# V as three one-pass products, graph 0 in another order, and L's first two tiles one behind the other

## What is computed

```python
def hypergraph_conv(x, adj, W, b):
    H = (adj != 0).astype(x.dtype)
    w = adj.reshape(N, -1)[:, :C]                 # the first row of adj
    xw = jnp.einsum('ncd,hd->nch', x, W)
    Dn = jnp.einsum('nce,ne->nc', H, w);  Dn = jnp.where(Dn > 0, 1.0 / Dn, 0.0)
    Be = H.sum(axis=1);                   Be = jnp.where(Be > 0, 1.0 / Be, 0.0)
    m = Be[:, :, None] * jnp.einsum('nce,nch->neh', H, xw)
    return Dn[:, :, None] * jnp.einsum('nce,neh->nch', H, m) + b

h = jax.nn.relu(hypergraph_conv(x, adj, W1, b1))
y = hypergraph_conv(layer_norm(h, gamma, beta), adj, W2, b2) + x
x = _layernorm(x + y)
agg = jnp.einsum('bij,bjf->bif', adj, x) / jnp.maximum(deg, EPS)
x = _layernorm(x + relu(concatenate([x, agg]) @ WL.T))
```

## Time and profile before

| | us |
|---|---|
| median of 3 runs | 1089.8 (1089.41 to 1090.03) |
| the profiled execution | 1090.12 |
| its span | 1088.5 |
| PE busy | 1073.5 (99%) |
| DVE, ACT, POOL busy | 746.4, 372.7, 217.5 |
| granted TensorE clock | 0.999 in the mean (2.4 GHz) |

### The profile page before, as it was taken

The page is one execution under the profiler, slowest core; times in us unless marked ns, Lnnn a source line. Parts: engine busy times, 40 slices in busy tenths (PEclk is TensorE's granted clock), DMA queues, the critical chain, the costliest instruction groups (busy, mean ns, idle before and its releaser), DMA issues.

```text
span 1088.5 us, 18849 instructions
## 1 busy us (share of the span) xinstructions
PE 1073.5 (99%) x6235; PEld 919.3 (84%) x6235; DVE 746.4 (69%) x1972; ACT 372.7 (34%) x811; POOL 217.5 (20%) x276
## 2 busy tenths in 40 slices
PE   7899999999999999999999999999999999999997
PEld 7789698896988969898798978989789896888966
DVE  6875596665965768758687486774867747867326
ACT  5372213622145321453115431154302533026230
POOL 1623004220041202312032120411204120041000
PEclk9999999999999999999999999999999999999999
DMA  8207712076210662125611355115542065300001
GB/s 295 59 1 156 155 42 57 0 154 155 57 40 24 130 157 55 39 54 121 143 48 39 83 126 117 41 39 112 128 87 68 9 142 127 68 11 1 1 1 39
DMA packets 63871, 86.44 MB, mean 79 GB/s; under 512 B 8164, under 2 KB 53864, under 8 KB 63848
## 3 DMA queue, kind: packets, MB, share of 16 engines
q1 hardware_dynamic: 63376, 85.75, 34.4%
q10 hardware_dynamic: 472, 0.40, 0.1%
HBM read 77.73 MB, written 8.39 MB: 79 GB/s over the span
## 4 chain that ended last, share of the span: by engine, by line
PE 91%; DVE 6%; DMA 1%; issue 1%; ACT 0%; SPq 0%; DVEq 0%
PE bank L882 41%; PE bank L993 10%; PE bank L1056 10%; PE bank L975 10%; PE bank L912 8%; PE bank L1023 3%; PE bank L1028 3%; PE bank L1029 3%; PE bank L1001 3%; PE bank L1041 1%; DMA raw<-in_adj_dram 1%; DVE adjT L666 1%; DVE unread L618 1%; DVE HT L671 1%; DVE m_lo L653 1%
## 5 line engine op out<-in xcount | busy, mean ns | idle before, releaser
L882 PE MATMUL bank<-yv,adjT 128*128 128x257 f32 x1024 | 223.3, 379 | 0.0
L882 PEld LDWEIGHTS bank<-yv,adjT 128*128 128x128 f32 x1024 | 193.6, 189 | 31.8 <-issue 3.8
L469 ACT ACTIVATE small<-mv,small 128x1 f32<-128x1 f32 x192 | 56.6, 295 | 348.8 <-DVE mv L648 248.8
L403 POOL TENSOR_TENSOR xres<-x_in 128x256 f32<-128x256 f32 x64 | 45.6, 748 | 410.3 <-DMA out_dram<-xres 406.8
L882 PE MATMUL bank<-x_hi,H 128*128 128x256 f32 x512 | 126.0, 287 | 0.0
L912 PE MATMUL bank<-x_hi,H 128*128 128x258 f32 x512 | 123.8, 289 | 1.9 <-DVE x_lo L702 1.4
L882 PE MATMUL bank<-x_lo,H 128*128 128x256 f32 x512 | 122.4, 280 | 0.0
L993 PE MATMUL bank<-gW2T,xnT 128*128 128x256 f32 x512 | 122.1, 381 | 0.0
L882 PE MATMUL bank<-m_hi,HT 128*128 128x256 f32 x512 | 121.6, 280 | 0.0
L882 PE MATMUL bank<-m_lo,HT 128*128 128x256 f32 x512 | 120.9, 279 | 0.0
L912 PE MATMUL bank<-x_lo,H 128*128 128x256 f32 x512 | 119.3, 282 | 0.1
(11 more groups left out here) (102 smaller groups left out, 1814.4 us busy)
## 6 DMA issues: line engine op xcount, KB each, us to landing
raw<-in_adj_dram SPq DMA_DIRECT2D x112, 256.0 KB, 8.6
adjB<-in_adj_dram SPq DMA_DIRECT2D x224, 128.0 KB, 3.4
x_in<-in_x_dram SPq DMA_DIRECT2D x31, 256.0 KB, 4.6
out_dram<-xres SPq DMA_DIRECT2D x108, 64.0 KB, 1.6
raw<-in_adj_dram SPq DMA_DIRECT2D x8, 512.0 KB, 10.4
w_row<-in_adj_dram SPq DMA_DIRECT2D x8, 512.0 KB, 3.7
out_dram<-xres SPq DMA_DIRECT2D x4, 256.0 KB, 2.2
W1n<-in_L_gnn_W_dram SPq DMA_DIRECT2D x1, 512.0 KB, 11.0
```

Of the source, the lines that this page charges most:

```text
L403: nc.gpsimd.tensor_tensor(xres[:, t, :], x_in[:, t, :], x_in[:, t, :], ALU.add).then_inc(xb_part, 1)
L469: nc.scalar.activation(std[:, i:i + 1], mv[:, which, i, 1:2], ACT.Sqrt, bias=eps_c)\
L882: last = mm(bank(stage, i)[:, 0:n_cols], lhsT, rhs, start=(k == 0 and part == 0), stop=(k == NT - 1 and part == parts - 1))
```

## The change

**V.** x1's transposed tile is taken as three parts: ACT makes x1_high (in x_hi's tiles 4 to 6) and a scaled copy, DVE makes x1_low from it and empties the bank (take_x1_low), POOL makes x1_cross. There are three slots of each. WL is split likewise in every graph behind take_m_hi of S3: WL_high and WL_cross's first step on ACT, WL_low and the subtraction on POOL, four operations of 512. PE's V(i) is four float32r products, VM(i) two, in banks of their own. ACT copies V(i) to yv with the factor 1 + 1/4096, DVE subtracts VM(i). TX(0) and TX(1) go ahead of S4's tile 6, TX(2) behind S4, TX(i+3) behind VM(i).

**Centring.** The first norm's centring goes from DVE to ACT (centre_rows), with a shift that POOL makes in two operations of 128x1 (shift_of); so does the second norm's in all graphs but the last.

**Next graph's work.** raw is loaded from P's last product on (its last quarter from Q's), its sums stand on DVE ahead of and behind take_q(7) and between S3's take_m_lo, five H tiles stand in S4's iterations 2 to 6 and three behind V. split_x_hi stands behind V, split_x behind the last H tile.

**L.** `group=1`: tile 0 with all its k, then tile 1.

**Graph 0.** Rows of adj are loaded ahead of weights; W1, W2 and WL are transposed at tiles 5, 6 and 7; the W1 splits go from POOL to DVE, behind sum_bW2; the sums go back behind S1 except for three; the rBe of six tiles are made at once; POOL's residual waits for the first z_cross.

The core of the diff:

```diff
+    "V": (4, 0, 2, 4, 0, 2, 4, 0),
+    "VM": (5, 1, 3, 5, 1, 3, 5, 1),
...
                 for i in range(NT):
+                    n = i % X1_SLOTS
                     pe.wait_ge(*free("V", i, b))
                     pe.wait_ge(*emptied("TX", i, b))
                     for d in range(ND):
-                        last = mm(bank("V", i)[:, :], x1T[:, i % 2, d, :], WLT[:, d, :],
+                        part = slice(d * P, (d + 1) * P)
+                        mm(bank("V", i)[:, :], x1_high[n][:, part], WL_high[:, d, :], start=(d == 0), stop=False)
+                        last = mm(bank("V", i)[:, :], x1_low[:, n, part], WL_low[:, d, :],
+                                  start=False, stop=(d == ND - 1))
+                    fills_bank(last, "V", i)
+                    pe.wait_ge(*free("VM", i, b))
+                    pe.wait_ge(x1_cross_done, b * NT + i + 1)
+                    for d in range(ND):
+                        last = mm(bank("VM", i)[:, :], x1_cross[:, n, d * P:(d + 1) * P], WL_cross[d],
                                   start=(d == 0), stop=(d == ND - 1))
-                    fills_bank(last, "V", i)
-                    if i + 2 < NT:
-                        transpose_x1(i + 2)
+                    fills_bank(last, "VM", i)
+                    if i + X1_SLOTS < NT:
+                        transpose_x1(i + X1_SLOTS)
...
+                for i in range(NT):
+                    root("1", 1, std_1, i, b)
+                    if i > 0:
+                        centre_rows("1", rstd_1, shift_1, shift_1_done, i - 1)
+                    if NT - 4 <= i < NT - 1:
+                        take_x1(i - (NT - 4))
+                centre_rows("1", rstd_1, shift_1, shift_1_done, NT - 1)
+                for i in range(NT):
+                    if i + 3 < NT:
+                        take_x1(i + 3)
+                    act.wait_ge(*full("V", i, b))
+                    empties_bank(nc.scalar.activation(yv[:, i, 0:2 * D], bank("V", i)[:, :], ACT.Copy,
+                                                      scale=1.0 + 1.0 / SPLIT), "V", i)
...
+                for i in range(NT):
+                    if i >= NT - 3:
+                        take_x1_cross(i - (NT - 3))
+                    shift_of("1", 1, rstd_1, shift_1, mean_1_scaled, shift_1_done, i, b)
+                for i in range(3, NT):
+                    take_x1_cross(i)
...
                 for i in range(NT + 1):
+                    if i in (NT - 2, NT - 1):
+                        take_x1_low(i - (NT - 2))
...
+                take_x1_low(2)
                 nc.vector.memset(yv[:, :, 2 * D:YP], 1.0).then_inc(y_ones, 1)
                 if more:
...
+                    build_rDn(b + 1)
+                for i in range(NT):
+                    dve.wait_ge(*full("VM", i, b))
+                    dve.wait_ge(*emptied("V", i, b))
+                    empties_bank(nc.vector.tensor_tensor(yv[:, i, 0:2 * D], yv[:, i, 0:2 * D], bank("VM", i)[:, :],
+                                                         ALU.subtract), "VM", i)
+                    if i + 3 < NT:
+                        take_x1_low(i + 3)
```

More of the change, by code:

```diff
@@ L193, in graph_net @@
         assert NT >= 2 * NH and at[0] <= nc.sbuf_usable_end, (at[0], nc.sbuf_usable_end)
-        banks = [ctx.enter_context(nc.psum_tensor(f"bank{n}", [P, 512], F32)) for n in range(N_BANKS)]
+        psum = ctx.enter_context(nc.psum_tensor("bank", [P, N_BANKS, 512], F32))
+        banks = [psum[:, n, :] for n in range(N_BANKS)]
         def sem(name):
@@ L563, in graph, with centre_rows @@
                     take_m_hi("S3", e, b, NT + e)
+                for d in range(ND):
+                    nc.scalar.activation(WL_high[:, d, :], WLT[:, d, :], ACT.Copy, scale=ROUND_DOWN)\
+                      .then_inc(WL_high_done, 1)
+                for d in range(ND):
+                    nc.scalar.activation(WL_cross[d], WLT[:, d, :].rearrange("p (a c) -> p a c", a=2), ACT.Copy,
+                                         scale=ROUND_DOWN / SPLIT).then_inc(WL_scaled, 1)
+                def centre_rows(norm, rstd, shift, done, i):
+                    act.wait_ge(done, b * NT + i + 1)
+                    nc.scalar.activation(xres[:, i, :], xres[:, i, :], ACT.Identity,
+                                         scale=rstd[:, i:i + 1], bias=shift[:, i:i + 1]).then_inc(normed[norm], 1)
@@ new lines, in take_x1 @@
+                def take_x1(i):
+                    n = i % X1_SLOTS
+                    act.wait_ge(*full("TX", i, b))
+                    nc.scalar.activation(x1_high[n], bank("TX", i)[:, 0:D], ACT.Copy, scale=ROUND_DOWN)\
+                      .then_inc(x1_high_done, 1)
+                    nc.scalar.activation(x1_cross[:, n, :], bank("TX", i)[:, 0:D], ACT.Copy, scale=SPLIT * ROUND_DOWN)\
+                      .then_inc(x1_scaled, 1)
+                for i in range(NT):
[4 more added lines that the diff above has]
+                        take_x1(i - (NT - 4))
@@ L565, in graph @@
                     split_x_hi(b + 1)
[L566 to L579, removed]
-                    if i + 2 < NT:
-                        take_x1T(i + 2)
                 for i in range(NT):
@@ L788, in graph, with next_Dn @@
                         take_q(s - LAG_Q - 1)
+                def next_Dn(tiles, into):
+                    if more:
+                        for c in tiles:
+                            sum_Dn(c, b + 1, into, (raw_loaded[c // 2], (b + 1) * IN_B))
+                next_Dn((0,), unread_Q)
                 take_q(NT - 1)
+                next_Dn((1, 2, 3), unread_Q)
                 if more:
```

198 lines of the change are left out of this document (132 added, 66 removed), and 1 row of the table PRODUCT_BANKS.

## The result

| | before | after |
|---|---|---|
| median, us | 1089.85 (1089.41 to 1090.03) | 1078.85 (1078.57 to 1079.16) |
| span of the profiled execution, us | 1088.5 | 1077.0 |

The ratio is 0.9901, 95% interval 0.9889 to 0.9913: faster by 11.0 us, where 6.6 were forecast.

A forecast was written before the change was run, and what follows sets the result against it. PE was taken as the bound: 1090.1 us for the profiled run, less 3.0 for V and S4 over eight graphs and 3.6 for graph 0, gave 1083.5, or 1083.2 against the median; range 1077 to 1094.

The forecast's parts named there:

- The bound and V's products: PE bounds; in V six one-pass products replace four pieces per tile, 11.14 instead of 13.76 us, -2.62 a graph.
- One wait, its place and its releaser: In V, PE waits 2.1 us once a graph before tile 5's transposes, until DVE has made x1_low(3).
- The 0.15 put on top for S4: In S4, 0.15 us added because DVE's iteration gets an H tile and POOL splits WL just then.
- The last graph: No H tiles or sums there, DVE is earlier, so the stall is 1.65 us and the gain -0.9.
- rival 2: POOL ends WL's split late in S4, past S4+7.9 each 0.1 us costs PE 0.1: 1092 to 1100 us, chance 0.14.
- POOL late with WL: POOL's four 512-wide operations in S4, forecast to end at S4+7.5, just in time; later makes it slower, chance 0.14.
- edge: In S4, the end of WL's split at S4+7.9, from which each further 0.1 us costs PE 0.1.
- Graph 0: M(0) 4.6 us earlier, M(4) held +1.0 by POOL's z_cross: -3.6 us, between -5 and 0.
- the end of the first six S1 tiles: In graph 0, PE ends them at about 28.4 us instead of 30.7: -2.3, estimated from two waits and the loads.
- The zeros: Moved work in S3 and L causes no PE wait, L's new order costs nothing, DVE's lag there matters nothing: zero.

The follow-up runs named there:

- x3_low: Changed kernel with ACT copying x1 tile 3 ahead of tile 7's centring and DVE making x1_low(i+3) ahead of VM(i)'s subtraction: 1067.0 us, ratio 0.9794.
- pool_twice: Changed kernel with two more 128x1 operations on POOL ahead of the shift of tile 7, read by nobody: 1092.4 us, ratio 1.0027.
- one_more_wl: Changed kernel with one more 512-column POOL operation between WL's low part and its cross part in each graph: 1092.5 us, ratio 1.0025.
- residual_early: Changed kernel with POOL's residual of graph 0 waiting for W1's split and DVE's last sum instead of the first z_cross: 1079.2 us, ratio 0.9905.
- no_stall_pool_twice: Changed kernel with ACT's tile 3 copies and DVE's x1_low moved ahead, plus two more 128x1 POOL operations before tile 7's shift: 1069.4 us, ratio 0.9813.
- low_first: Changed kernel with DVE making x1_low(i+3) ahead of the subtraction of VM(i) instead of behind it: 1070.6 us, ratio 0.9827.

## Why the prediction was right, and where its sizes were off

**The bound and V's products: right.** The forecast took PE as the bound and 27.97 us from S4 to L without a wait; x3_low shows 27.97.

**One wait, its place and its releaser: right. Its size: 1.54, not 2.1.** PE got there at T+4.83 (forecast T+4.87) and went on at T+6.37, not T+6.95. Link by link, ends as forecast and as in the rows above:

| end, us behind T | forecast | measured |
|---|---|---|
| last eviction, its start | 0.63 | 0.31 |
| aggregate | 1.95 | 1.51 |
| reciprocal | 2.46 | 2.04 |
| x1_cross(2) | 3.72 | 3.18 |
| shift | 3.96 | 3.59 |
| centring | 4.54 | 4.23 |
| copies of tile 3 | 5.19 | 4.77 |
| V(0) copied | 5.79 | 5.26 |
| x1_low(3) | 6.90 | 6.32 |

Three terms were mis-sized. x1_low(1) was begun at T, not after it, and lets the eviction start 0.31 later: 0.32 early. The sum laid durations end to end, while an operation on ACT or DVE starts about 0.1 before the shown end of the one ahead: centring to first copy is 0.51 for a duration of 0.60, copy to copy 0.26 for 0.36. That is about 0.5 over the chain. Against it, POOL's small operations were dearer: 0.19 each and 0.26 from start to start, so 0.41 for the pair where 0.24 was taken, inside the stated 0.10 to 0.30; and the centring took 0.60, not 0.50. The 0.15 put on top for S4 was 0.07. Together 0.65 us a graph, in seven graphs 4.6 us. The last graph was forecast with a wait of 1.65 and -0.9, and has 1.52 and -0.98.

**A cost that the forecast didn't have.** Its own 2.1 us is a wait behind which, by pool_twice, the clock would have dropped in six graphs of eight, and by one_more_wl, whose wait is a little longer, in two of seven. Taken at its word the forecast's mechanism gives about 1083.2 + 2 x 1.6 = 1086 to 1083.2 + 6 x 1.6 = 1093, an estimate, where before has 1089.85. The chain came out 0.56 shorter, and nothing of this shows: that was luck. The sign of the change hung on half a microsecond, which rival 2's 0.14 did not express. The range, up to 1094, would have held it, but for another reason: its upper part was put there for POOL's lateness.

**POOL late with WL: rightly a rival, and rightly not the forecast.** Its four operations:

```profile
489.55 3.47 POOL L445 TENSOR_TENSOR WL_low<-WLT,WL_high 128x512 fp32r<-128x512 f32 x2 [11.31 <-ACT WL_high L610]
492.97 2.36 POOL L450 TENSOR_TENSOR x_hi<-x_hi,WL_low 128x512 fp32r<-128x512 f32 x2
...
1014.65 2.55 POOL L445 TENSOR_TENSOR WL_low<-WLT,WL_high 128x512 fp32r<-128x512 f32 x2 [11.76 <-ACT WL_high L610]
```

They end at S4+7.06 (forecast 7.5, edge 7.9). The first pair lies beside a sum on DVE (489.38 to 490.60) and takes 3.47; in the last graph, which has no sums, the same pair takes 2.55. So one sum costs POOL 0.9 us. The rule of the Trainium skill's GPSIMD Engine Reference, section Key points, that the prediction set against the change thus holds here, at 0.9 us for one sum; residual_early shows it from the other side, DVE slowed by POOL. An H tile costs POOL something too: in one_more_wl, where the last pair lies beside one, it takes 2.81 us instead of 2.36. The price that rival 2 put on a late split doesn't follow from its own edge: at 1.6 us an operation it has 31.4 us from S4 to L, while 4 x 1.6 from S4+1.3, with the 1.0 for Dn(7) that its 7.5 contains, ends at S4+8.7 and by its rule gives 30.2 + 0.8 = 31.0.

**Graph 0: -2.8, not -3.6.** PE begins M(0) and M(4) in after at:

```profile
46.08 0.74 PE L1140 MATMUL bank<-W_cross,z_cross 128*128 128x512 f32 x2 [1.06 <-DVE z_cross L844]
...
58.90 0.74 PE L1140 MATMUL bank<-W_cross,z_cross 128*128 128x512 f32 x2 [0.65 <-POOL z_cross L437]
```

45.2 and 58.1 were forecast; the 12.8 between them was forecast as 12.9. The term that was off is the end of the first six S1 tiles, 29.8 instead of 28.4. Some 0.6 of that is a wait which the forecast hadn't seen: PE's transposes of raw wait for a bank that ACT empties (27.27) behind W_high's two operations (1.15 us together, from 26.23). The rest is in the estimate for the loads, and in part it is spread: of the eight other kernels whose graph 0 is the same as after's, M(0) begins at 45.33 in the earliest (one_more_wl) and at 46.24 in the latest (no_stall_pool_twice), with 12.43 to 12.48 us from S2's start to M(0) in each, so this spread lies in S1 and its loads. From the six tiles on M(0) came 16.3 later, 16.8 were forecast.

**The zeros.** L takes 27.56 us before and after, S3 and S4's start are where the sum had them, and no wait stands in S3. Two gains were not foreseen: S2 of graph 1 is 0.4 shorter (11.64 before, 11.24 now), and S1 takes 15.33 instead of 15.44. The latter can't be credited to the change: S1 takes either 15.33 to 15.34 us or 15.43 to 15.45, and in one kernel both occur. After has the short one in all seven graphs behind the first, low_first and no_stall_pool_twice in two each, residual_early in one, and all other kernels of this study, the one before too, in none. What sets it is open.

**The sum as measured**: V 7 x 0.95 + 0.98 = 7.6, graph 0 2.8, S1 7 x 0.11 = 0.8, S2 0.4, less 0.2 at the end: 11.4 of the span's 11.5 us.

## What to carry to other kernels

When work is moved off the engine that bounds, write down the chain over the other engines in the order of their queues, and look in it for links that have no data in common: here two such links, one instruction's place each, were worth 12 us of a possible 20. Sum such a chain from start to start, not by durations, since an error of 0.1 us counts once per link and round. And price a wait of the matrix engine twice, by its length and by the clock behind it: 0.27 us more of it in each graph cost 2.9 us in all, 0.54 us more cost 13.6. Compare kernels stage by stage as well as by their time: here a stage that nobody touched and the loads of graph 0 moved by up to 0.9 us, and hid a gain of half a microsecond.

## What the runs showed of the hardware

- The granted clock of TensorE, at 1.00 until then, fell to 0.5 (1.2 GHz) for 3.4 us behind a wait of 2.08 us in six of eight graphs and behind one of 2.28 us in two of seven; behind waits of 1.54 and 1.81 us in none of eight. What tells the six from the two isn't known; where in this range it begins was not tried further.
- POOL took 0.19 us for an operation of 128x1, 0.26 from start to start; the tiny operation costs a third of one 256 wide (0.64 to 0.75).
- DVE and POOL slow each other. On POOL, WL's first pair of operations took 3.47 us beside a sum and 2.55 beside none. On DVE, small operations suffer too: 0.17 became 0.54 us for a 128x8 beside POOL's 256-wide residual.
